# Patch embedding as one FP32 product instead of a three-term FP16 split

## The reference, cut to what matters

```python
# x: (32, 3, 224, 224) -> 256 patches of 588 values per image; W: (256, 588)
h = einsum('bpk,ek->bpe', patches, W) + b                  # patch embedding
h = h + attn(layernorm(h))     # 16 heads of 16, 4 key/value heads, rotary, causal
h = h + ffn(layernorm(h))      # 704 wide, inputs, weights and activations quantised to 8 bits
```

## Time and profile before

| | us |
|---|---|
| median of 3 runs | 829.83 (829.82 to 830.21) |
| the profiled execution | 827.3 |
| its span in the trace | 825.6 |

### The profile page before, as it was taken

How to read it: one execution, slowest core, us unless ns; L and a number is a source line. 1 busy time by engine, 2 the same in 40 slices (tenths; PEclk the granted TensorE clock), 3 DMA queues, 4 the chain that set the end, 5 groups by cost and what they waited for, 6 DMA issues and landing times. The chain is left out here.

```text
span 825.6 us, 20928 instructions
## 1 busy us (share of the span) xinstructions
PE 666.7 (81%) x6706; PEld 381.5 (46%) x6706; DVE 663.3 (80%) x1052; ACT 586.9 (71%) x972; POOL 591.5 (72%) x689
## 2 busy tenths in 40 slices
PE   3578888888888888888888888888776369997894
PEld 2344555554555555545555555455333223332563
DVE  5856888888888888888888888888765359999894
ACT  4346677777777777787777777877666258886883
POOL 1456888888888888888888888886654148884363
PEclk9797999999999999999999999999889769999898
DMA  8245666667666655566665655665543212221499
GB/s 278 58 97 114 127 138 135 123 135 138 140 134 146 143 133 121 132 139 140 134 144 144 133 121 132 140 140 103 104 77 62 61 38 52 49 40 25 71 177 160
DMA packets 245384, 96.57 MB, mean 117 GB/s; under 512 B 222432, under 2 KB 240608, under 8 KB 245344
## 3 DMA queue, kind: packets, MB, share of 16 engines
q1 hardware_dynamic: 236896, 87.69, 48.3%
q0 software_dynamic: 8448, 8.39, 6.9%
HBM read 24.74 MB, written 16.78 MB: 50 GB/s over the span
## 5 line engine op out<-in xcount | busy, mean ns | idle before, releaser
L1198 DVE TENSOR_REDUCE act_all<-pair 128x4 f16<-128x1024 f32 (+1 forms) x192 | 234.2, 1220 | 34.5 <-PE pair L535 34.4
L484 PE MATMUL pair<-act_all 128*128 128x256 f16 (+1 forms) x960 | 116.7, 275 | 21.1 <-DVE act_all L1245 18.5
L829 ACT ACTIVATE act_all<-pair 128x768 f32<-128x768 f32 x128 | 103.0, 805 | 32.2 <-PE pair L552 32.2
L979 POOL TENSOR_SCALAR_AFFINE_SELECT ffn<-ffn 128x512 f32<-128x512 f32 x128 | 93.8, 742 | 42.4 <-ACT ffn L829 39.6
L829 ACT ACTIVATE ffn<-pair 128x768 f32<-128x768 f32 x128 | 102.1, 797 | 19.1 <-PE pair L552 19.1
L979 POOL TENSOR_SCALAR_AFFINE_SELECT act_all<-act_all 128x512 f32<-128x512 f32 x128 | 78.4, 633 | 43.2 <-ACT act_all L829 43.2
L484 PEld LDWEIGHTS pair<-act_all 128*128 128x128 f16 (+1 forms) x960 | 90.1, 98 | 40.0 <-issue 22.6
L550 PE MATMUL pair<-act_all 64*128 64x256 f16 x512 | 72.6, 280 | 39.7 <-ACT ffn L829 24.3
L1184 DVE TENSOR_TENSOR act_all<-act_all 128x512 f16<-128x512 f32 x32 | 69.8, 2181 | 41.2 <-ACT act_all L822 41.2
L991 POOL TENSOR_TENSOR act_all<-act_all 128x160 f32<-128x160 f32 x128 | 76.4, 618 | 27.2 <-ACT act_all L791 27.2
L1011 POOL TENSOR_TENSOR act_all<-act_all 128x1280 f16<-128x1280 f32 x31 | 81.4, 2627 | 18.0 <-ACT act_all L781 18.0
(11 more groups left out here) (135 smaller groups left out, 1510.9 us busy)
## 6 DMA issues: line engine op xcount, KB each, us to landing
act_all<-x_t SPq DMA_DIRECT2D x32, 640.0 KB, 4.2
out<-act_all SPq DMA_DIRECT2D x32, 256.0 KB, 2.6
out<-ffn POOLq DMA_DIRECT2D x16, 512.0 KB, 7.0
act_all<-act_all SPq DMA_TRANSPOSE x192, 3.0
act_all<-w_down SPq DMA_DIRECT2D x1, 704.0 KB, 8.4
act_all<-w_emb SPq DMA_DIRECT2D x1, 640.0 KB, 3.9
ffn<-w_gate SPq DMA_DIRECT2D x1, 640.0 KB, 6.9
ffn<-w_up SPq DMA_DIRECT2D x1, 640.0 KB, 7.5
```

What stands on the lines that cost most here:

```text
L484: mm = pe.matmul(b, xs[0:k, sx, c, tb * P:(tb + 1) * P], we[0:k, sw, c, :], start=(c == 0 and (sx, sw) == PARTS[0]), stop=(c == KC - 1 and ...
L829: act.activation(probs[i // 4][:, o:o + 2, 0:3, :].rearrange("p h k s -> p h (k s)"), pair[1][:, :].rearrange("p (h c) -> p h c", h=2)[:, ...
L979: pool.affine_select(out=p, in_=p, pattern=[[0, 4], [1, P]], compare_op=ALU.is_ge, fill=0.0, base=0, channel_multiplier=-1).then_inc(maske ...
L1198: dve.tensor_reduce(to, pair[2][:, :].rearrange("p (k g t) -> p k g t", k=2, g=n_), AX.X, ALU.max).then_inc(unit_reduced, 1)
```

## The change

`patch` multiplies the loaded FP32 patches by the loaded FP32 weights directly: 5 matmuls for each half in the code. The splits of patches and weights on ScalarE, GpSimd and VectorE go, as does the scaling by 64 of the weights and its inverse in `embedded`. SP's `next_x` waits for the patch product instead of the splits.

```diff
-        x_parts = [part(2 * KC * TOKENS, FP16)... for _ in range(2)]
-        we = part(2 * KC * D, FP16).rearrange("p (s c e) -> p s c e", s=2, c=KC)
+        we = part(KC * D).rearrange("p (c e) -> p c e", c=KC)
...
-            sp.dma_start(raw_we, w_emb).then_inc(emb_loaded, 16)
+            sp.dma_start(we, w_emb).then_inc(emb_loaded, 16)
...
             def next_x(n):
-                sp.wait_ge(x_high_ready, n - 1)
-                sp.wait_ge(x_low_ready, n - 1)
+                sp.wait_ge(done["patch"], n - 1)
                 load_x(n % 2, n)
...
                 if x.known and z.n == 0 and tb == 0:
-                    pe.wait_ge(weights_split, 1)
+                    pe.wait_ge(emb_loaded, 16)
                 if tb == 0:
-                    pe.wait_ge(x_high_ready, z.n + 1)
-                    pe.wait_ge(x_low_ready, z.n + 1)
-                xs = x_parts[z.parity]
+                    pe.wait_ge(xt_loaded[z.parity], z.half * 16 + 16)
                 for c in range(KC):
                     k = P if c < KC - 1 else K_LAST
-                    for sx, sw in PARTS:
-                        mm = pe.matmul(b, xs[0:k, sx, c, tb * P:(tb + 1) * P], we[0:k, sw, c, :],
-                                       start=(c == 0 and (sx, sw) == PARTS[0]),
-                                       stop=(c == KC - 1 and (sx, sw) == PARTS[-1]))
+                    mm = pe.matmul(b, xt[z.parity][0:k, c, tb * P:(tb + 1) * P], we[0:k, c, :],
+                                   start=(c == 0), stop=(c == KC - 1))
...
-            def x_high(x):                      # ScalarE, and its call after exp_pair 3
-                ...
-                act.activation(x_parts[v.parity][:, 0], xt[v.parity], ACT.Copy).then_inc(x_high_ready, 1)
...
-            def x_low(v):                       # GpSimd, and its call between masks 4 and 5
-                ...
-                pool.tensor_tensor(x_parts[v.parity][:, 1], xt[v.parity], x_parts[v.parity][:, 0],
-                                   ALU.subtract).then_inc(x_low_ready, 1)
...
-            weights_low(1, we, raw_we)          # VectorE, at the start
-            dve.wait_ge(x_high_ready, 1)
-            dve.tensor_tensor(x_parts[0][:, 1], xt[0], x_parts[0][:, 0], ALU.subtract).then_inc(x_low_ready, 1)
```

More of the change, by code:

```diff
@@ L160, in vit_layer @@
         xt = [part(KC * TOKENS).rearrange("p (c t) -> p c t", c=KC) for _ in range(2)]
-        x_parts = [part(2 * KC * TOKENS, FP16).rearrange("p (s c t) -> p s c t", s=2, c=KC) for _ in range(2)]
-        we = part(2 * KC * D, FP16).rearrange("p (s c e) -> p s c e", s=2, c=KC)
+        we = part(KC * D).rearrange("p (c e) -> p c e", c=KC)
         wqkv = part(2 * DC * QKV_COLS, FP16).rearrange("p (s c e) -> p s c e", s=2, c=DC)
         wo = part(2 * DC * D, FP16).rearrange("p (s c e) -> p s c e", s=2, c=DC)
[L168 to L171, removed]
+        raw = act_all[:, NG * A_COLS - DC * QKV_COLS - DC * D:NG * A_COLS]
+        raw_wqkv = raw[:, 0:DC * QKV_COLS].rearrange("p (c e) -> p c e", c=DC)
+        raw_wo = raw[:, DC * QKV_COLS:DC * QKV_COLS + DC * D].rearrange("p (c e) -> p c e", c=DC)
         h_parts = part(2 * TB * D, FP16).rearrange("p (s e) -> p s e", s=2)
@@ L258, in vit_layer @@
         weights_split = sem("weights_split")
-        x_high_ready = sem("x_high_ready")
-        x_low_ready = sem("x_low_ready")
         on_high_ready = sem("on_high_ready")
@@ L475, in patch @@
                 if x.known and z.n == 0 and tb == 0:
-                    pe.wait_ge(weights_split, 1)
+                    pe.wait_ge(emb_loaded, 16)
                 if tb == 0:
-                    pe.wait_ge(x_high_ready, z.n + 1)
-                    pe.wait_ge(x_low_ready, z.n + 1)
-                xs = x_parts[z.parity]
+                    pe.wait_ge(xt_loaded[z.parity], z.half * 16 + 16)
                 for c in range(KC):
                     k = P if c < KC - 1 else K_LAST
-                    for sx, sw in PARTS:
-                        mm = pe.matmul(b, xs[0:k, sx, c, tb * P:(tb + 1) * P], we[0:k, sw, c, :],
-                                       start=(c == 0 and (sx, sw) == PARTS[0]),
-                                       stop=(c == KC - 1 and (sx, sw) == PARTS[-1]))
+                    mm = pe.matmul(b, xt[z.parity][0:k, c, tb * P:(tb + 1) * P], we[0:k, c, :], start=(c == 0),
+                                   stop=(c == KC - 1))
                 if tb == TB - 1:
@@ L494, in project @@
                 if x.known and z.n == 0 and tb == 0:
-                    pe.wait_ge(weights_split, 3)
+                    pe.wait_ge(weights_split, 2)
                 for c in range(DC):
@@ L766, in embedded @@
                 fence(act)
-                act.activation(h_of(z), shared[JOBS.index(("patch", 0)) % 2][:, :],
-                               ACT.Copy, scale=1.0 / W_UNIT).then_inc(read["patch"], 1)
+                act.activation(h_of(z), shared[JOBS.index(("patch", 0)) % 2][:, :], ACT.Copy).then_inc(read["patch"], 1)
                 wait(act, h_turned[z.parity - 1], (z + -1).half * 16 + 16)
@@ L772, in embedded @@
                 act.activation(h_parts[:, 0], h_of(z), ACT.Copy).then_inc(h_high_ready, 1)
-            def x_high(x):
[L776 to L780, removed]
-                act.activation(x_parts[v.parity][:, 0], xt[v.parity], ACT.Copy).then_inc(x_high_ready, 1)
             def projected(x, tb):
@@ L859, in weights_turned_copy @@
                 op.then_inc(weights_ready, 1)
[L861 to L864, removed]
             act.wait_ge(consts_loaded, CONSTS)
@@ L889, in step @@
                     exp_pair(late, 3)
-                if (x + 4).exists():
-                    x_high(early)
                 if (x + -2).exists():
@@ L1005, in add_rotated @@
                                    rot_b[:, tb].rearrange("p h d -> p (h d)"), ALU.add).then_inc(qk_ready, 1)
-            def x_low(v):
-                if v.known and v.n == 0:
-                    return
-                pool.wait_ge(x_high_ready, v.n + 1)
-                pool.tensor_tensor(x_parts[v.parity][:, 1], xt[v.parity], x_parts[v.parity][:, 0],
-                                   ALU.subtract).then_inc(x_low_ready, 1)
             def power(ready, n, to, of, signal, rows=None):
@@ L1032, in step @@
                     mask(late, 4)
-                if (x + 4).exists():
-                    x_low(early + 3)
                 if (x + -1).exists():
@@ L1147, in _ @@
             op.then_inc(centred, 1)
-            weights_low(2, wqkv, raw_wqkv)
-            weights_low(3, wo, raw_wo)
+            weights_low(1, wqkv, raw_wqkv)
+            weights_low(2, wo, raw_wo)
             dve.wait_ge(sig_ready, 1)
```

## The result

The changed kernel takes 834.02 us (median of 7 runs, 832.28 to 835.45), the kernel before 829.82 in the same comparison: a ratio of 1.0052, 95% interval 1.0036 to 1.0069. It is slower by half a per cent; forecast was 828.0. The profiled execution took 832.84, with a span of 830.8 (before 825.6).

What follows compares the result with a forecast made beforehand. Two branches race to `residual`; the change shortens the first, lengthens the second, which then ends last. -3.5 + 1.2 = -2.3 us gives 825.0 profiled; the median is 2.5 above, 827.5, given as 828.0; range 819 to 840.

Steps and rivals of the forecast that it cites:

- -3.5 us for 25 steps: Loop from 100.14 to 559.04 us: each of 25 steps 0.14 us shorter, 18.24 instead of 18.38.
- +0.7 at the start: Image 2 on TensorE: FP32 product +1.05 us, of which 0.35 idle before 46.38 hides some.
- +0.5 at the end: Last `patch`, step from 559.04: it had no split beside it, so 17.65 us becomes 18.2.
- Two branches: First: `attend`, GpSimd's rotations, `high`, `low`, ending last. Second: `o_normalise`, `patch`, `out_project`, 0.41 us to spare. Both release `residual`.
- the rule cited in the prediction: TensorE weight loads overlap matmuls only where row groups differ; by it 20 loads would add 2.8 us to each image.
- the sum for a step: TensorE's chain from `patch` 0 at 7.50 through `out_project` 14.65 and `residual` 16.37 to the next step at 18.24 us.
- Before: 18.38: Step length of the kernel before, start to start of `unit_pair` 1, against which 18.24 was 0.14 us less.
- It costs nothing now and gives nothing: ScalarE's split, 1.26 us, is followed by a 1.57 us wait for the rotations; removing it only lengthens that wait.
- the second branch: `o_normalise` on VectorE, then TensorE from `patch` to `out_project`, releasing `residual`; 0.56 us longer per half of `patch`, ending last.
- the rival with that branch off the path: `patch` half costs at most 0.2 us extra; ScalarE and GpSimd set 17.65 us steps: 811, halfway 819; chance 0.17.
- The ends: Outside the 25 steps: image 0 counted 0, image 2 +0.7, images 3 and 4 0, last `patch` +0.5; +1.2 us.
- The new waits cost nothing: SP's `next_x` waiting for `patch` and TensorE's wait for loaded patches add no time in the loop.

Runs made afterwards that it cites:

- the one with both sides long: The changed kernel with both splits of the patches put back in their old places as unused work: 835.33 us, ratio 1.0084 to the kernel before.
- changed, again: The changed kernel run once more with nothing altered, for the spread of the start between executions: 833.43 us.

## Why the prediction was wrong

It said 828.0 and more likely faster; the kernel is slower. The terms of the sum were -3.5 us for 25 steps, +0.7 at the start and +0.5 at the end; measured are +1.2, +3.9 and +0.1.

**Right: the mechanism of the step.** Two branches meet in `residual`. GpSimd's split cost its time through VectorE; without it `low` fell by the 2.18 us that the earlier trace rows promised, `out_project` took over as the last release, TensorE has no idle time before `score_pair` 5 and 6, and ScalarE's wait before `high` grew to 2.22 us. The run without GpSimd's split (17.96) and the one with both sides long (18.39) bear it out.

**Right: what an FP32 product costs.** Ten instructions for a half, which with the change of jobs take 2.35 us; 2.31 was forecast, from instructions of 0.213 us (they start 0.215 to 0.216 apart). The weight loads are hidden, as assumed and against the rule cited in the prediction (the Trainium skill's "TensorE: Matmul & The Clock Gate", Part 3, "The mechanism"): the group of them shows 0.194 us each, and not the 0.14 of L581, 1.94 us for a half, inside these 2.35.

```profile
L476 PEld LDWEIGHTS pair<-act_all 128*128 128x128 f32 x512 | 94.4, 194 | 36.8 <-issue 18.0 <-DVE act_all L1208 3.6 <-ACT act_all L758 1.2
```

**Wrong: the size of "the sum for a step".** Forecast 18.24, measured 18.37. `patch` 1 follows 2.95 us behind `patch` 0 (2.89 forecast), `score_pair` 5 2.36 behind that (2.31), each later distance is 0.01 to 0.02 longer; `patch` 0 starts 0.04 earlier. Together +0.12 in the step shown. And "Before: 18.38" was the longer one of the two steps of a pass; their mean is 18.34. A gain of 0.14 us a step was a difference of two numbers near 18.3 with 0.13 and 0.04 of error in them; it is a loss of 0.03. That makes 25 x 0.17 = 4.3 us of the miss; the other 0.4 of the steps' part are single steps, the one of 19.33 here against one of 18.68 (from 173.53) in before.

**Wrong: "It costs nothing now and gives nothing", of ScalarE's split.** It was worth 0.18 us a step with GpSimd's split in place, and its place about 0.1 with GpSimd's in pieces. This did not move the result, since the second branch ends last, but the rival with that branch off the path had its floor wrong: 17.86 in the loop, not 17.65, with ScalarE's exponential ahead of `score_pair` 6 as what sets it.

**Wrong: "The ends", at the start.** The term of +0.7 us priced the products of the first images as 20 x 0.213 against 30 x 0.107, nothing for image 0 and 0.7 for image 2. The earlier trace rows shows 4.32 and 4.02 us for 30 FP16 instructions, where 30 x 0.107 are 3.2: the start was already slower than this price. In the changed kernel images 0 and 2 take 1.88 and 1.58 us more (0.94 and 1.11 in its second execution, "changed, again" in the table above). In image 2 the instructions start 0.43 us apart up to 45.10, at a granted clock of 0.50, and 0.215 apart behind that. The first `unit_pair` 1 comes 2.1 us later by this (0.7 in the second execution).

The rest, 1.8 us (3.9 in the second execution), hangs on two things that no term held. The change takes instructions out of TensorE's program, the 16 KB packets that bring it come at other moments, and some of them meet the transposes that TensorE waits for; and the granted clock falls at other moments too. With the same products and 128 idle waits, the regular steps began at 98.61, earlier than before's 100.14; with a packet among the transposes at about 60 us, at 102.85 to 105.00 (four executions with whole products in the start and no splits). How much of the 0.5% is the product's own stays open: the loop gives 0.03 us a step, 0.8 us in all; at the start the products could not be separated from the place of the program and the clock.

"The new waits cost nothing" was nearly right: at the start SP did wait, 3.6 us, and loaded image 4's patches at 48.60 instead of 44.10, but its next job, at 54.79, was not ready before that; in the loop this wait does not show.

## What to carry to other kernels

Where two chains meet, work taken off the one is worth only the slack of the other; compute both to a tenth of what you hope to gain, over a whole period of the loop, and when they are that close forecast no change. Before paying for a cheaper split on the busy engine, look at where the split stands: moving the two splits to other places in their engines' lists gained 1.6% here, and replacing them gained nothing. When a change alters how many instructions an engine runs, time a copy with idle instructions added as well; what that moves is not the change's.

## What the runs showed of the hardware

- A packet of 16 KB of an engine's program takes 0.9 to 2.0 us in these traces (0.88 at 65.07), and DMA transposes in flight then land later: 3.4 us in the median and not 2.6. A step that met one was up to 1.7 us longer (16.89 for 15.16 in the FP32 kernel, 18.86 for 18.29 in the FP16 one), or no longer at all: in the kernel before one falls at 152.26 us into transposes from 149.70 on, and the step takes 18.31.
- A VectorE operation of 512 elements that takes 0.69 us alone takes 2.44 beside a GpSimd operation of 2.63 that started before it; where VectorE's operation starts first, GpSimd's add of 0.86 us takes 1.28 (311.24).
- An FP32 product of 256 columns by 128 x 128 weights takes two instructions, which start 0.215 us apart at the granted clock of 1.00 and 0.43 apart at 0.50; the two weight loads of 0.194 us hide behind them at 1.00.
